# Differential attention and routed experts on one core: VectorE's side work one step at a time, q and k in halves, another order on SyncE's queue

## What is computed

```python
q = rope((x @ Wq).reshape(B, T, 32, 4));  k = rope((x @ Wk).reshape(B, T, 16, 4));  v = (x @ Wv) ...
# 16 heads, 2 of them share k and v; each head has two score maps j = 0, 1
attn = softmax(causal(q1 k1^T / 2)) @ v - lambda_full * softmax(causal(q2 k2^T / 2)) @ v
attn = attn / rms(attn) * rms_w * (1 - LAMBDA_INIT)
x = layernorm(x + attn.reshape(B, T, 128) @ Wo)
route = softmax(x @ router_w + router_b);  e = argmax(route)
x = layernorm(x + (silu(x @ w1a[e]) * (x @ w1b[e])) @ w2[e] * max(route))
```

## Time and profile before

| | us |
|---|---|
| median of 3 runs | 728.77 (726.62 to 730.02) |
| profiled execution, device time | 732.72 |
| its span | 730.9 |
| TensorE busy (matmuls) | 614.7 |
| VectorE busy | 544.5 |
| ScalarE busy | 428.4 |
| GpSimd busy | 392.4 |
| phases 0 to 7, 31.2 to 154.1 us of the span | 122.9 |
| phases 8 to 27, 154.1 to 470.1 us | 316.0 |
| phases 28 to 31, 470.1 to 530.4 us | 60.3 |
| the rest, with phases 32 and 33 | 200.5 |

### The profile page before, as it was taken

The page is one execution under the profiler, slowest core; times in us unless marked ns, Lnnn a source line. Parts: engine busy times, 40 slices in busy tenths (PEclk is TensorE's granted clock), DMA queues, the critical chain, the costliest instruction groups (busy, mean ns, idle before and its releaser), DMA issues.

```text
span 730.9 us, 18729 instructions
## 1 busy us (share of the span) xinstructions
PE 614.7 (84%) x6744; PEld 329.8 (45%) x6744; DVE 544.5 (74%) x1310; ACT 428.4 (59%) x889; POOL 392.4 (54%) x576
## 2 busy tenths in 40 slices
PE   3388789979989988999898899989986994999990
PEld 1123334434443443344344334434433884899980
DVE  6587668867898897789789788979944777466660
ACT  1106568857776775777677577758764351344430
POOL 6244025644676576467657546521744077577764
PEclk9558999999999999999999999989999998899995
DMA  3867634643762674265266436523016454365530
GB/s 108 260 214 234 219 114 155 229 121 109 231 199 85 203 232 141 83 220 195 85 209 223 141 97 204 185 81 100 20 52 218 157 166 136 121 209 193 178 120 22
DMA packets 73364, 114.52 MB, mean 157 GB/s; under 512 B 20028, under 2 KB 43068, under 8 KB 72988
## 3 DMA queue, kind: packets, MB, share of 16 engines
q1 hardware_dynamic: 64200, 87.23, 37.8%
q0 software_dynamic: 5808, 23.24, 9.2%
q10 hardware_dynamic: 3264, 2.85, 1.2%
HBM read 69.60 MB, written 47.27 MB: 160 GB/s over the span
## 4 chain that ended last, share of the span: by engine, by line
PE 61%; DVE 14%; issue 8%; ACT 4%; DMA 4%; SPq 3%; another core or an unknown queue 3%; POOL 2%; POOLq 0%; ACTq 0%; DVEq 0%
PE bank L683 17%; PE bank L811 11%; DVE mr L1347 6%; PE bank L823 4%; PE bank L640 4%; PE bank L613 4%; PE bank L595 4%; ACT work L883 3%; PE bank L604 3%; PE bank L622 3%; PE bank L631 3%; PE bank L720 2%; DMA qk_apart<-apart 1%; PE bank L739 1%
## 5 line engine op out<-in xcount | busy, mean ns | idle before, releaser
L1347 DVE TENSOR_REDUCE mr<-bank 128x8 f32<-128x512 f32 x576 | 357.4, 683 | 82.3 <-PE bank L613 49.9
L883 ACT ACTIVATE work<-bank 128x512 f32<-128x512 f32 x576 | 313.2, 600 | 101.0 <-PE bank L640 66.0
L683 PE MATMUL bank<-work,v_aug 128*32 128x512 f32 (+7 forms) x2048 | 177.6, 432 | 0.0
L613 PE MATMUL bank<-rows 64*128 64x384 bf16 (+7 forms) x512 | 145.1, 296 | 0.0
L604 PE MATMUL bank<-rows 64*128 64x128 bf16 (+7 forms) x512 | 143.5, 297 | 0.0
L640 PE MATMUL bank<-qd,kz 64*128 64x384 bf16 (+7 forms) x512 | 140.6, 290 | 0.0
L631 PE MATMUL bank<-qd,kz 64*128 64x128 bf16 (+7 forms) x512 | 136.7, 288 | 0.0
L595 PE MATMUL bank<-bits 64*128 64x128 bf16 x448 | 100.2, 226 | 16.6 <-DVE mr L1347 12.6
L622 PE MATMUL bank<-bits 64*128 64x128 bf16 x448 | 98.7, 224 | 17.4 <-ACT work L883 9.2
L595 PEld LDWEIGHTS bank<-bits 64*128 64x128 bf16 x448 | 41.7, 94 | 126.8 <-DVE mr L1347 111.4
L1076 POOL CAST msplit<-mt 128x32 bf16<-128x32 f32 x32 | 7.6, 239 | 169.0 <-DVE mt L1357 117.5
(11 more groups left out here) (176 smaller groups left out, 952.7 us busy)
## 6 DMA issues: line engine op xcount, KB each, us to landing
qk_apart<-apart SPq DMA_DIRECT2D x96, 256.0 KB, 3.1
rows<-qk_apart SPq DMA_DIRECT2D x64, 192.0 KB
kz<-qk_apart SPq DMA_DIRECT2D x64, 192.0 KB
qk_parts<-parts SPq DMA_DIRECT2D x90, 128.0 KB, 2.7
rows<-qk_parts SPq DMA_DIRECT2D x64, 96.0 KB
qd<-qk_parts SPq DMA_DIRECT2D x64, 96.0 KB
x_sorted<-in_c_pad SPq DMA_DIRECT2D x9, 390.0 KB, 4.2
xr<-x_sorted SPq DMA_DIRECT2D x23, 130.0 KB
```

The source lines that it names most:

```text
L613: pe.matmul(bk[:, wa:T], qz[lo:lo + L, kv, i - 1].rearrange("p j l -> p (j l)"), kd[lo:lo + L, kv, 0:T - wa], start=False, stop=True, skip ...
L683: m = pe.matmul(pv_b[32 * t:32 * t + 32, L * kb:T], v_aug[:, vb, kv + v, kb, :], cols, start=kb == 0, stop=True, skip_group_check=True)
L883: nc.scalar.activation(prob[:, pos, r, :], st_b[no % ST_RING][:, :], ACT.Exp, scale=HD ** -0.5).then_inc(s_sfree, 1)
L1347: V.tensor_reduce(mr[:, s % 2, u % 2, i, i:i + NB], nat_b[no % NAT_RING][:, :].rearrange("p (n t) -> p n t", t=L), AX.X, ALU.max)\
```

## The change

- VectorE's side work is cut into single steps, one behind each maximum, by the table `JOBS` (phases after the batch's first, first tile, number of steps) and `jobs_at(g, u)`. `weigh` does its reciprocal in two halves. `take` keeps what empties a bank; the rest is in `stats`, `choose`, `chance_of` and `place_of`.
- q and k are projected by halves of 256 columns, in two slots and two banks each (q: phase A, slots 2 and 6; k: B, slots 2 and 8); ScalarE copies each half out. v goes from slot 5 to 8.
- `CHAIN` is spread differently: turn_attn (A, 8), wo (B, 6), norm (C, 1), turn_x1 (C, 4), router (C, 6), chances (C, 8), rank (A, 4), sort (A, 6). It begins two phases earlier.
- GpSimd: `turn` of the next batch moves from phase A to D before it; `inverse_root` and `rms_norm` move to slots 6 and 7 of D.
- SyncE: row operands are loaded one phase ahead instead of two, key operands in the phase before their use instead of three before it; `kd` stands ahead of `max_in` instead of behind the stores; the stores of a batch are spread over four phases, six in each.

```diff
-BATCH_USES = [(6, "q", -4), (6, "k", -3), (5, "v", -2)]
+BATCH_USES = [(2, "q", -4), (6, "q2", -4), (2, "k", -3), (8, "k2", -3), (8, "v", -2)]
-CHAIN = {"turn_attn": (10, 6), "wo": (10, 8), "norm": (11, 0), "turn_x1": (11, 6), "router": (11, 8),
-         "chances": (12, 1), "rank": (12, 3), "sort": (12, 6)}
-CHAIN_SHORT = {"turn_attn": (8, 4), "wo": (8, 6), "norm": (9, 0), "turn_x1": (9, 4), "router": (9, 6),
-               "chances": (9, 7), "rank": (9, 8), "sort": (9, 8)}
+CHAIN = {"turn_attn": (8, 8), "wo": (9, 6), "norm": (10, 1), "turn_x1": (10, 4), "router": (10, 6),
+         "chances": (10, 8), "rank": (12, 4), "sort": (12, 6)}
+CHAIN_SHORT = {"turn_attn": (8, 2), "wo": (8, 4), "norm": (8, 5), "turn_x1": (9, 1), "router": (9, 3),
+               "chances": (9, 4), "rank": (9, 6), "sort": (9, 7)}
+JOBS = {"weigh": (6, 12, 3), "guess": (7, 8, 5), "stats": (9, 14, 6), "choose": (10, 14, 8), "chance": (11, 14, 2),
+        "place": (12, 10, 3)}
+JOBS_SHORT = {"stats": (8, 9), "choose": (9, 7), "chance": (9, 12), "place": (9, 13)}
+
+def jobs_at(g, u):
+    for b in range(B - 1):
+        for name, (lag, first, steps) in JOBS.items():
+            if b == B - 2 and name in JOBS_SHORT:
+                lag, first = JOBS_SHORT[name]
+                if (SUPER * b + lag, first) == (g, u):
+                    for k in range(steps):
+                        yield name, b, k
+            else:
+                k = (g - SUPER * b - lag) * NU + u - first
+                if 0 <= k < steps:
+                    yield name, b, k
...
             for g in range(PHASES):
...
+                if g + 1 < NS:
+                    row_operands(g + 1, qz)
                 if 0 <= g - 1 < NS:
                     max_out(g - 1)
-                if g + 2 < NS:
-                    row_operands(g + 2, qz)
+                if g + 1 < NS:
+                    row_operands(g + 1, kd)
                 if 0 <= g - 1 < NS:
                     max_in(g - 1)
-                if g + 1 < NS:
-                    key_operands(g + 1)
-                for a in range(2):
-                    b = batch_of(g, a - 3)
-                    if b:
-                        write_parts(sp, b, a)
-                        write_apart(sp, b, a)
-                if g + 2 < NS:
-                    row_operands(g + 2, kd)
+                    key_operands(g - 1)
+                if g == 0:
+                    write_parts(sp, 0, 0)
+                if batch_of(g, -3):
+                    write_apart(sp, batch_of(g, -3), 0)
+                if batch_of(g, -2):
+                    write_parts(sp, batch_of(g, -2), 1)
+                if batch_of(g, -1):
+                    write_parts(sp, batch_of(g, -1), 0)
+                if batch_of(g, 0) is not None:
+                    write_apart(sp, batch_of(g, 0), 1)
...
-            def project(a, bk):
+            def project(a, bk, cols):
...
+                    pe.matmul(bk[lo:lo + 32, cols], wq_s[:, 2 * a, lo:lo + 32], xr[:, 2 * f, cols], start=True, stop=False)
...
+            for i in range(4):
+                turn(1, i)
             for g in range(PHASES):
...
-                    b = batch_of(g, -4)
+                    b = batch_of(g, -5)
                     if b and 1 <= t < 5:
                         turn(b, t - 1)
...
                     b = batch_of(g, 7)
-                    if b is not None and t == 3:
+                    if b is not None and t == 6:
                         inverse_root(b)
-                    if b is not None and t == 5:
+                    if b is not None and t == 7:
                         rms_norm(b)
...
             for g in range(PHASES):
-                for t in range(NC):
+                for u in range(NU):
                     if g < NS:
-                        row_max(g, 2 * t)
-                        row_max(g, 2 * t + 1)
-                    for name, n in uses(g, t):
-                        take(name, n)
-                        if name == "rank" and n in GROUP_BATCH:
-                            group(GROUP_BATCH.index(n))
...
+                        row_max(g, u)
+                    if u % 2:
+                        for name, n in uses(g, u // 2):
+                            take(name, n)
+                    for name, b, k in jobs_at(g, u):
+                        job(name, b, k)
```

More of the change, by code:

```diff
@@ L518, in _ @@
             row_operands(0, kd)
-            row_operands(1, qz)
-            row_operands(1, kd)
-            write_parts(sp, 0, 0)
-            write_apart(sp, 0, 1)
-            sp.wait_ge(s_kclear, 2)
-            for r in range(2):
-                sp.dma_start(kz[L * r + MROW:L * r + MROW + 6, :, :, :, :].rearrange("p k n j l -> p (k n j l)"),
-                             c_minus).then_inc(s_minus, 16)
-            key_operands(0)
             for g in range(PHASES):
@@ L763, in _ @@
             pe.wait_ge(s_xr, 4)
-            project(0, banks[0]).then_inc(s_first, 1)
-            project(1, banks[1]).then_inc(s_first, 1)
+            for a in range(2):
+                project(a, banks[a], slice(0, T)).then_inc(s_first, 1)
             pe.wait_ge(s_wv, 16)
@@ L1297, in _ @@
             first_apart(1, 2)
+            NH = NI * KVH * 2
             def head_constants():
@@ new lines, in weigh @@
+            def weigh(b, k):
+                if k < 2:
+                    emptied(dve, "turn_ot", SUPER * b + SUPER - 1)
+                    i = slice(NI // 2 * k, NI // 2 * k + NI // 2)
+                    V.reciprocal(rl[:, 2 * NH // 2 * k:2 * NH // 2 * (k + 1)],
+                                 on_s[:, i, :, :, :].rearrange("p i k r (j v) -> p (i k r j) v", v=VW)[:, :, 2 * HD])\
+                        .then_inc(s_rl, 1)
+                else:
+                    wait(dve, s_rl, 3 * b + 2)
+                    second = rl[:, :].rearrange("p (n j) -> p n j", j=2)[:, :, 1]
+                    V.tensor_scalar(second, second, lam_n[:, 0:1], None, ALU.mult).then_inc(s_rl, 1)
@@ L1407, in rank_of @@
[L1407 to L1424 removed]
+                else:
+                    if n in GROUP_BATCH:
+                        V.tensor_copy(total[:, n - GROUP_BATCH[0], :], bk[:, NI * NX:NI * NX + NX]).then_inc(s_total, 1)
+                    V.tensor_tensor(coded[:, :, :], bk[:, 0:NI * NX].rearrange("p (i e) -> p i e", i=NI),
+                                    over(io_region, BT, 1), ALU.add).then_inc(free, 1)
@@ new lines, in chance_of, with place_of @@
+            def chance_of(b, k):
+                wait(dve, s_rt, RT_STEPS * b + 8 + k)
+                if k == 0:
+                    wait(dve, s_rexp, b + 1)
+                    V.tensor_reduce(rsum[:, :], chance[:, :, :], AX.X, ALU.add).then_inc(s_rt, 1)
+                else:
+                    V.reciprocal(x1_all[:, NI * b:NI * b + NI, E], rsum[:, :]).then_inc(s_rt, 1)
+            def place_of(b, k):
+                wait(dve, s_rt, RT_STEPS * b + 10 + k)
+                if k == 0:
+                    emptied(dve, "rank", b)
+                    V.tensor_tensor(place_f[:, :, :], coded[:, :, :], chosen[:, b % 2, :, :], ALU.mult)\
+                        .then_inc(s_rt, 1)
+                elif k == 1:
+                    V.tensor_reduce(pos_f[:, :], place_f[:, :, :], AX.X, ALU.add).then_inc(s_rt, 1)
+                else:
+                    V.tensor_copy(pos_u[:, NI * b:NI * b + NI], pos_f[:, :]).then_inc(s_pos, 1)
+                    if b in GROUP_BATCH[:2]:
+                        group(GROUP_BATCH.index(b))
@@ L1426, in _, with job @@
+            def job(name, b, k):
+                if name == "weigh":
+                    weigh(b, k)
+                elif name == "guess":
+                    first_guess(b, k)
+                elif name == "stats":
+                    stats(b, k)
+                elif name == "choose":
+                    choose(b, k)
+                elif name == "chance":
+                    chance_of(b, k)
+                else:
+                    place_of(b, k)
             group_steps = [0]
@@ L1587, in _ @@
             gate(0)
-            weigh(b7)
+            for k in range(JOBS["weigh"][2]):
+                weigh(b7, k)
             last_difference()
             gate(1)
-            first_guess(b7)
+            for k in range(JOBS["guess"][2]):
+                first_guess(b7, k)
             last_rms()
@@ L1595, in _ @@
             take("wo", b7)
+            for k in range(JOBS["stats"][2]):
+                stats(b7, k)
             last_variance()
@@ L1602, in _ @@
             take("router", b7)
+            for k in range(JOBS["choose"][2]):
+                choose(b7, k)
             mix(3)
             gate(5)
+            for k in range(JOBS["chance"][2]):
+                chance_of(b7, k)
             take("rank", b7)
+            for k in range(JOBS["place"][2]):
+                place_of(b7, k)
             mix(4)
```

159 lines of the change are left out of this document (72 added, 87 removed).

## The result

The changed kernel takes 760.92 us (median of 5 runs, 750.93 to 769.17) where the kernel before took 730.02 (726.62 to 731.26): a ratio of 1.036, 95% interval 1.031 to 1.041. Forecast was 714. The profiled execution (device time 769.17, span 767.2 us) is one of two slow ones of the five, which the ratio leaves out; so I use its rows for mechanisms and the ratios for prices, and e13, the same kernel in an execution of 735.91 us, as a check on its rows.

A forecast was written before the change was run, and what follows sets the result against it. No engine is always busy; the limit alternates, TensorE in B, VectorE in D. Gains of 9.9 (early phases), 0 (steady groups), 2.6 (phases 28 to 31) and 2.0 (phase 33), 14.5 us, take 728.8 to 714; range 700 to 730.

The forecast's parts named there:

- A: Phase number modulo 4 = 0, taken as TensorE's, with 3.3 us charged to four indirect stores: 16.8 us becomes 17.4.
- B: Phase number modulo 4 = 1, bounded by TensorE; wo and halves added: 13.9 us becomes 15.3.
- C: Phase number modulo 4 = 2, the longest: 17.3 us, less 2.1 of burst, plus 1.8 waiting for the norm, gives 17.0.
- D: Phase number modulo 4 = 3, bounded by VectorE: 15.0 us becomes 14.3, with 0.4 for the lock 14.7.
- part (1): SyncE's new queue order: keys land about 13 us into each phase; phases 2, 3, 4 and 7 shorten, 9.9 us gained.
- rival 3: Keys land too late, from about 14.3 us on; phases wait at the boundary, 26 us more, 740 us; chance 0.08.
- The lead: TensorE's lead left by D, up to four banks of 0.62 us, half counted: 1.2 us off the load added to A and B.
- Rival 2: GpSimd overflows C, so split_max and the keys come late: 2.5 us a group more, 727 us; chance 0.18.
- part (2): VectorE's single steps behind each maximum remove bursts: 2.1 us at C's end, 1.9 at D's end.
- The lock: VectorE's five two-tensor steps of choose wait for GpSimd's running operation: 0.5 us each, 0.4 us charged to D.
- Phases 28 to 31: Phases without split, turn or projection, hence no norm wait or lock: 60.3 us becomes 57.7, 2.6 gained.
- The tail: Phase 33, rank at slot 6 instead of 8, so group arithmetic and first transposed rows come earlier: 2.0 us gained.

The follow-up runs named there:

- e13: The changed kernel itself, unaltered, timed again on another chip: 738.33 us, ratio 1.045 to the kernel before.
- e2: The kernel before with only SyncE's new queue order, keys loaded in the phase before their use: 731.36 us, ratio 1.033.
- e4: The kernel before with SyncE's new queue order, but keys loaded a phase earlier than in the change: 701.78 us, ratio 0.989.
- e3: The changed kernel with only the keys loaded a phase earlier: 723.75 us, ratio 1.021.
- e12: e5 with the rank at slot 6 and the sort at slot 8 of A instead of 4 and 6: 722.07 us, ratio 1.019.
- e15: e5 with the chain a slot earlier, rank and sort left at slots 4 and 6 of A: 704.96 us, ratio 0.994.
- e16: e3 with all five steps of the first guess together in unit 8 of D: 712.44 us, ratio 1.006.
- e5: e4 plus VectorE's single steps behind each maximum, with the chain in its old phases: 723.61 us, ratio 0.986.
- e18: e16 with turn_x1, router and choose two slots later: 703.16 us, ratio 0.991.
- e6: e4 plus only q and k projected by halves: 723.27 us, ratio 0.989.
- e7: e4 plus only the chain's new slots, VectorE's bursts kept: 738.04 us, ratio 1.006.
- e8: e7 plus GpSimd's turn moved to D and the root's products at slots 6 and 7 of D: 755.34 us, ratio 1.032.
- e17: e3 with the first guess's single steps beginning at unit 2 of D instead of 8, beside the turn: 713.57 us, ratio 1.006.

## Why the prediction was wrong

**The step that failed** is in part (1): "So the keys land about 13 us into each phase", and from it "a phase without other work can't be shorter than some 14 us" with 9.9 us gained in the early phases. The landing is right for the D phases only (12.7 to 14.3 us), and 15.9 in phase 2, where the store of the maxima alone takes 4.3 us to land. Worse, the test was wrong: I held the landing against the phase's length, while TensorE wants the keys of a D phase at 11 to 12 us. So rival 3, at 0.08, is what happened with the queue, and its threshold of 14.3 us was some 3 us too late for D. Its price of 26 us was close: e2 has 31.1 us of key waits and is 23 us slower than before. e2 and e4, which differ in these lines alone, show it.

**The lead.** In the sum I credited A and B with 1.2 us, since D would leave TensorE a lead. D came at the forecast or below (13.2 us in the window, 13.2 to 14.8 in all; forecast 14.7), but all five end in a wait for keys: A is 16.9 to 20.0 us (phases 8 to 24) where 17.4 was forecast, B 15.4 to 18.5 for 15.3. That the lead is paid behind D is seen best in e2 and e4, which differ in the keys alone: D is 15.0 us in both, A 15.4 against 14.2 in the mean and B 15.0 against 14.4. Not all of A's length in the changed kernel's trace is this. The forecast's A has 3.3 us in it for which no releaser is named; the trace above has 2.2 to 3.1 us of such waits of ScalarE in phases 16, 20 and 24; and e13, on a chip whose traces have none (last section), has an A of 14.8 to 17.4 us.

**Rival 2's cover.** I wrote that if split_max were late, "VectorE holds four banks of 0.6 us then, which covers it". It doesn't: e3 has 17.0 us of these waits, e12 20.3, and e15 and e16 show that removing them pays 2.2% and 1.5%. In the changed kernel itself little of it shows (0.8 us, and 3.1 in e13), as the keys hold TensorE up first. I also looked for the overflow in C. It comes at the end of D, since part (2) costed the guess's steps on VectorE alone, and not for GpSimd, which waits for the last of them.

**C.** The wait for the norm was forecast at 1.8 us and is 1.8:

```profile
472.04 1.08 PE L758 MATMUL bank<-ident,x_all 128*128 128x128 f32 x4 [1.77 <-POOL x_all L1163]
```

But C was forecast at 17.0 and is 18.6 in e3 (phase 18), without any key wait, with VectorE busy 15.7 us there. The 2.1 us of the burst, which I subtracted in full, were not all to be had: e5, which takes it away with the chain in its old phases, has a C of 15.9 where e4 has 17.3, 1.4 us less. The rest is not resolved. That the wait and what stands behind it cost more than 1.8 us is seen in e18, whose C is 4.3 us shorter than e16's.

**The lock** was sized well. I took 0.5 us for each of five steps; the less step averages 1.27 us and is the worst. VectorE and GpSimd in phase 22:

```profile
409.89 1.63 DVE L1437 TENSOR_TENSOR less<-logit,rmax 128x32 f32<-128x32 f32 x1
...
412.05 0.82 DVE L1440 TENSOR_TENSOR coded<-logit,rmax 128x32 f32<-128x32 f32 x1
```

```profile
409.51 1.96 POOL L1114 TENSOR_TENSOR at<-on_s,rl 128x1024 f32<-128x1024 f32 x1 [1.06 <-issue]
411.55 1.26 POOL L1123 TENSOR_TENSOR dif<-at 128x512 f32<-128x512 f32 x1
```

Each ends with GpSimd's product. Over the 8 batches the means are 1.27, 0.66, 0.49, 0.18 and 0.42 us for less, coded, place_f, chosen and cnt, 2.1 us a batch more than 0.18 each. `place_f` of the rank is at 0.18 in all cases, as said. The halves, forecast at 0.2 us a phase, can't be told from nothing (e6).

**Phases 28 to 31** were to gain 2.6 us: 60.3 to 57.7. That gain was never there: the window of the earlier trace rows runs 2.6 us past the last maximum. Up to it before takes

```profile
470.10:527.80 57.70, 52.08 (x676) 22.85 (x668) 50.79 (x101) 42.00 (x85) 21.55 (x42) 0.94 0.27 77
```

and the changed kernel 62.2, since 28 to 30 end in waits for keys. **The tail** was to gain 2.0 and loses 4.3 in the profiled execution. The gap for the rank did shrink as forecast, from 5.26 to the second line here, and from the last exponential on the kernel takes 2.2 us less. But ahead of it the chain that ended last has the first line, a wait that names nobody in the program, in which neither ScalarE nor VectorE works, while GpSimd issues indirect transfers:

```profile
581.76 5.78 another core or an unknown queue
...
597.31 3.34 issue
```

And TensorE ran 13.7 us at the lower clock there. This is the stretch from the first exponential of phase 33 to the last, 20.9 us where before takes 14.1:

```profile
575.30:596.20 20.90, 16.78 (x148) 7.26 (x147) 5.84 (x32) 10.95 (x22) 10.02 (x11) 0.67 0.56 194
```

**Open.** Of the 1.7% that the chain's new slots cost in e7, the wait for x_all (13.9 us in six waits) is seen; e4 was not run on that chip, and e6, which was, has the halves besides. What the unnamed wait of 5.78 us in the tail is, no run shows; e13, on another chip, has a tail 8.2 us shorter. How much of the loss is the clock that falls after a wait, and how much the wait, was not separated.

## What to carry to other kernels

A load that goes from slack to none must be held against the moment at which its reader asks for the data, not against the stage's end. An engine that runs ahead of the others asks earlier, and the lead that it loses is paid in the next stages. When work is spread into single steps, ask who waits for the last step: five steps behind five maxima hand their result over 2 us later than in one go (3.5 us from the first to the last in e3, 1.5 in e16), and GpSimd, which waits for it, was late for everything that followed. Two lost slacks hide each other: mending one paid 1.3 or 2.4%, mending both 5.5 to 6%.

## What the runs showed of the hardware

- The 3.3 us for which VectorE stood in A with no releaser named, charged to the four stores, depend on the chip too. Where before takes 731 us such waits are there in all four, e5, e6 (first line below, VectorE's waits), e7 and e8. On the four chips where it takes 707 to 709 us none of the 14 traces has one of over 1.5 us; e4 issues the same stores in the same slot, and its A takes 14.1 us (second line, window of phase 20):

```profile
DVE mr L1349 <- remote: 8.8, 3, 3.0
```

```profile
328.50:342.60 14.10, 13.08 (x179) 5.12 (x170) 13.25 (x27) 10.44 (x23) 9.89 (x12) 1.00 0.66 209
```

- The granted clock. In e3 phase 22 took 21.0 us, phase 18 with the same work and the same wait for x_all 18.6. Of phase 22 TensorE spent 11.4 us at the lower of the two levels (1.2 of 2.4 GHz), of phase 18 nothing. The window of phase 22 shows 0.73:

```profile
367.60:388.60 21.00, 19.03 (x189) 9.96 (x181) 15.98 (x33) 11.39 (x24) 16.22 (x20) 0.73 0.48 149
```

  Both phases had a wait of 1.8 us in them, so that wait alone doesn't decide it.
- One-tensor steps of VectorE are locked beside GpSimd's products as two-tensor ones are (e8, e17, e18). The trace of before had it in small, and I overlooked it: beside GpSimd's `x_all` (L1140) the step `nv` took 0.39 us in six of the eight batches, and 0.20 in the other two.
